# Graph network on one core: a landing wait, the place of a store, and the form of the one-hots

## What is computed

```python
# layer 0: Gaussian mixture convolution
gauss  = exp(sum(-0.5 * (attr - mu)**2 / (eps + sigma**2)))      # 3 weights per edge
msg    = einsum('eko,ek->eo', (x[src] @ g).reshape(E, 3, 64), gauss)
summed = segment_sum(msg, dst);  cnt = segment_sum(1, dst)
h      = summed / max(cnt, 1) + x @ root_w + bias
x      = layernorm(x + silu(h + x))
# layer 1: two SAGE convolutions over the same edges
h      = relu(x @ W_self1 + mean_of_neighbours(x) @ W_neigh1 + b1)
h      = h @ W_self2 + mean_of_neighbours(h) @ W_neigh2 + b2
out    = layernorm(x + h)
```

## The kernel before

| stretch | us | tiles q | counts are made by |
|---|---|---|---|
| first | 370 to 2099 | 0 to 29 | alternately two pairs a window (L1266, L1268), and merged (L1395, L1396) |
| second | 2099 to 2899 | 30 to 45 | one pair a window; many windows listed |
| third | 2899 to 3701 | 46 to 61 | one pair a window |
| fourth | 3701 to 5434 | 62 to 97 | merged; DVE also merges for the next tile (L1359 to L1376, with copies by ACT, L563) |

## Time and profile before

### The profile page before, as it was taken

How to read it: one execution, slowest core, us unless ns; L and a number is a source line. 1 busy time by engine, 2 the same in 40 slices (tenths; PEclk the granted TensorE clock), 3 DMA queues, 4 the chain that set the end, 5 groups by cost and what they waited for, 6 DMA issues and landing times.

```text
span 7415.5 us, 142564 instructions
## 1 busy us (share of the span) xinstructions
PE 4994.0 (67%) x35195; PEld 3986.1 (54%) x35196; DVE 4364.1 (59%) x15089; ACT 2698.4 (36%) x8317; POOL 3383.0 (46%) x3146
## 2 busy tenths in 40 slices
PE   1566666666655666666655555555645999999999
PEld 1223334443433444444444444444434999999999
DVE  5667888788877777676666665666634222222222
ACT  3113455454443455444455555555522000000000
POOL 5023666666665667677666666666610000000000
PEclk5557898888877888787777777788865999999999
DMA  2001222222222222222222222222220999999998
GB/s 74 28 25 48 92 75 91 86 79 75 91 73 89 82 101 92 74 92 92 79 89 93 93 93 93 93 75 93 93 67 35 368 381 381 382 369 386 384 385 342
DMA packets 258225, 1081.29 MB, mean 146 GB/s; under 512 B 140103, under 2 KB 144231, under 8 KB 194407
## 3 DMA queue, kind: packets, MB, share of 16 engines
q1 hardware_dynamic: 142806, 968.66, 33.9%
q0 software_dynamic: 100352, 102.96, 6.1%
q10 hardware_dynamic: 14902, 8.11, 0.5%
HBM read 751.67 MB, written 327.81 MB: 146 GB/s over the span
## 4 chain that ended last, share of the span: by engine, by line
PE 34%; POOL 20%; issue 16%; DVE 15%; DVEq 8%; DMA 4%; ACT 2%; SPq 0%; POOLq 0%; ACTq 0%
PE pw L968 21%; POOL rE L500 20%; PE pw L795 5%; DVE rE L1268 4%; DMA rE<-in_x,idx 3%; PE pw L820 2%; DVEq L1477 2%; DVEq L1301 2%; PE pw L767 2%; DVE rE L1266 2%; DVE rE L1328 1%; PE pw L935 1%; ACT rE L547 1%; DVEq L1253 1%; DVE rE L1396 1%
## 5 line engine op out<-in xcount | busy, mean ns | idle before, releaser
L500 POOL DMA_INDIRECT rE<-in_x,idx x3136 | 3380.8, 1078 | 2028.8 <-issue 1885.9
L795 PE MATMUL pw<-rE 128*128 128x193 f32 x7824 | 1708.9, 380 | 842.6 <-DVE rE L1328 805.7
L586 ACT CAST rB<-pw 128x792 bf16<-128x792 f32 x1568 | 1262.2, 813 | 2689.1 <-PE pw L820 1039.0
L795 PEld LDWEIGHTS pw<-rE 128*128 128x128 f32 x7824 | 1561.0, 225 | 1050.9 <-DVE rE L1328 986.3
L547 ACT ACTIVATE rE<-rE,cols 128x64 f32<-128x64 f32 x4704 | 1254.8, 344 | 8.0 <-DMA tab<-tab_d 8.0
L820 PE MATMUL pw<-rE 128*128 128x396 f16 x3840 | 813.1, 359 | 532.8 <-DVE rE L1268 389.7
L1268 DVE TENSOR_SCALAR rE<-iperm,gr 128x392 f16<-128x392 f16 x3840 | 1049.0, 313 | 0.0
L820 PEld LDWEIGHTS pw<-rE 128*128 128x128 f16 x3840 | 368.5, 103 | 915.8 <-DVE rE L1268 501.7
L968 PE MATMUL pw<-rE,rA 128*128 128x192 bf16 x9604 | 809.5, 246 | 0.1
L968 PE MATMUL pw<-rB,rA 128*128 128x192 bf16 x9604 | 809.2, 246 | 0.1
L968 PEld LDWEIGHTS pw<-rE,rA 128*128 128x128 bf16 x9604 | 789.7, 98 | 1.4
(11 more groups left out here) (257 smaller groups left out, 2615.7 us busy)
## 6 DMA issues: line engine op xcount, KB each, us to landing
rA<-count SPq DMA_DIRECT2D x392, 1568.0 KB, 8.4
count<-rB SPq DMA_DIRECT2D x98, 3136.0 KB
rE<-in_x,idx POOLq DMA_INDIRECT x3136
cols<-cols_d SPq DMA_DIRECT2D x98, 64.0 KB
cols_d<-rA SPq DMA_DIRECT2D x3, 1568.0 KB, 5.1
rA<-in_edge_attr ACTq DMA_DIRECT2D x1, 4608.0 KB
out<-gcol ACTq DMA_DIRECT2D x97, 32.0 KB, 6.1
count<-rB SPq DMA_DIRECT2D x8, 224.0 KB, 2.0
```

The costliest lines, as they stand in the source:

```text
L500: pool.indirect_dma_start(out=gath[:, s, u * CB + b, :], out_offset=None, in_=x, in_offset=bass.IndirectOffsetOnAxis(ap=idx[:, s, u * CB + ...
L586: act.copy(stage[:, s, :, j * 2 * W:(j + 1) * 2 * W].rearrange("p h (w n) -> p w h n", w=2), pu[j % 3][:, :, 0:CW].rearrange("p w (h n) -> ...
L795: ins = pe.matmul(sums[side][:, 0:AW], onehot[:, side, bb, :], wgath[:, side, bb, :], start=(bb == 0), stop=(bb == CB - 1))
```

## The change

Three edits.

1. POOL waits for landed rows once per tile, after chunk 3, and no more after chunk 1.
2. SP stores the counts of tile q last in its step: after weights, table and indices, and thus also after all gathers of tile q+1 have landed.
3. In the 68 tiles from q = 30 (`pairs_w == 1`, and `behind < 2` in the merged ones from q = 62) each one-hot set is made by eight `tensor_scalar`, each comparing `iota` with one value per partition. Tiles 0 to 29 keep the single instruction.

```diff
@@ sync @@
             for q in range(NT):
...
-                sp.wait_ge(a_evac, q * NU + (NU + 2))
                 sp.wait_ge(a_bnd, q + 1)
-                sp.dma_start(tile_of(count[part][0], ORDER[q] - PARTS[part][0]), stage[:, q % 2, None, 0:NT, :]).then_inc(a_st[q % 2], 16)
                 if q + 2 < NT:
                     sp.wait_ge(a_list, q + 1)
                     load_cols(q + 2)
-                if q + 3 < NT:
+                if q + 1 < NT:
                     for u in range(U):
                         sp.wait_ge(a_g[1 - q % 2][u], 16 * CB * ((q + 1) // 2 + 1))
+                if q + 3 < NT:
                     load_idx(q + 3)
+                sp.wait_ge(a_evac, q * NU + (NU + 2))
+                sp.dma_start(tile_of(count[part][0], ORDER[q] - PARTS[part][0]), stage[:, q % 2, None, 0:NT, :]).then_inc(a_st[q % 2], 16)
@@ gpsimd @@
-                        if u % 2:
+                        if u == U - 1:
                             pool.wait_ge(a_g[s][u], 16 * CB * (i + 1))
@@ vector @@
-            def prepare(t, s, u):
+            def prepare(t, s, u, apart=False):
...
-                    V.tensor_tensor(onehot[:, side], iota[:, None, :].broadcast_to([P, CB, P]),
-                                    local[:, :, None].broadcast_to([P, CB, P]),
-                                    ALU.is_equal).then_inc(a_oh[side], 1)
+                    if apart:
+                        for bb in range(CB):
+                            ins = V.tensor_scalar(onehot[:, side, bb, :], iota[:], local[:, bb:bb + 1], None, ALU.is_equal)
+                    else:
+                        ins = V.tensor_tensor(onehot[:, side], iota[:, None, :].broadcast_to([P, CB, P]),
+                                              local[:, :, None].broadcast_to([P, CB, P]), ALU.is_equal)
+                    ins.then_inc(a_oh[side], 1)
@@ merged_counts @@
-                            prepare(q, s, u)
+                            prepare(q, s, u, behind < 2)
@@ tile_counts @@
-                            prepare(q, s, u)
+                            prepare(q, s, u, pairs_w == 1)
```

## The result

The changed kernel takes 7461.66 us (median of 6 runs, 7455.13 to 7465.4) against 7431.97 before: ratio 1.004, 95% interval 1.003 to 1.0051. It is 30 us slower, where 33 us less was forecast; the change is 0.4%, small but clear of the interval. A second set of runs on another chip gave 1.0048 (1.0031 to 1.0065).

The account below looks back on a forecast made before the run. POOL's gathers were taken to bound the third and fourth stretches, DVE and PE the second, with DVE the bound after the change. Terms +41 - 17 - 57 = -33 us took the median from 7427.8 to 7395 us, range 7310 to 7480.

Parts of the forecast that it names:

- Now the sets: Step adding 0.57 us for each of 72, 77 and 202 one-hot sets to DVE's chain: +41, +44, +115 us.
- Edit 1 on POOL: Pause after chunk 1 falls from 2.77 to 0.30: 2.5 us per tile off POOL, 40 and 90 us in stretches three, four.
- Edit 3 on POOL: Gathers held less by one-hot sets: 1.1 us a tile gained on POOL, 18 and 40 us in stretches three and four.
- Edit 3 on DVE: Eight comparisons cost DVE +0.57 us a set: +0.44 for the instructions, +0.13 for gathers hitting them; bounds +0.3 to +1.4.
- DVE's chain without POOL's stalls: DVE's waits replaced by their unstalled values: 741 us in the third stretch, 1561 in the fourth, L1248 doubtful by 40 us.
- Fourth stretch: From tile 62, 36 tiles: DVE's 1676 us against POOL's 1603, so 1733 becomes 1676, -57 us.
- Second and third: Stretches from tiles 30 and 46: second +41 us to about 841, third -17 us, from 802 to 785.
- Edit 2: The store moved last in SP's step, costed at nothing; 14 us of gathers cover it before `stage` is needed.
- rival 3: Store comes too late and `stage` isn't free; with 3 us in each of 52 tiles 7551 us; chance 0.03.
- Rival 1: POOL stays the bound, DVE's chain ending before POOL's: -147 us, 7281; chance 0.13.
- Rival 2: Comparisons and gathers hold each other up; change turns slower at 0.66 us a set, 7511 at 0.9; chance 0.20.
- Which is late next: Step comparing DVE's and POOL's chains: DVE last in both, 785 against 744 (third stretch), 1676 against 1603 (fourth).

Follow-up runs that it names:

- single form: The changed kernel with edits 1 and 2 only, every one-hot set made by one instruction as before: 7286.89 us, ratio 0.9815 to before on an undisturbed chip.
- the lagged one: Kernel with edits 1 and 2 and old one-hots, but POOL's wait at a tile's end is for chunk 2's rows: 7211.27 us, ratio 0.9709.

## Why the prediction was wrong

**The missing term.** The step "Now the sets" counts on DVE's chain only the sets, and the sum +41 - 17 - 57 has no term for what seven instructions more in four calls do to the loop they stand in. It was put at nothing without a reason. The runs show in its place 3.2 us more at the loop's head in each pass, 101 us in all, and 117 us by the difference between 341 and 348 instructions. Without it the measured kernel would be near 7462 - 117 = 7345 (an estimate), some 87 us under before and 50 below the forecast; with it, it is 30 over before. It could have been found: the queue's row stands in the profile of before (139), the single-pair loop already waited 1.9 and 5.0 us at its head, and the order of instructions shows the length of the body.

Its other steps, one by one:

- *Edit 1 on POOL*, -2.5 us a tile. Right, -2.2: in the single form the tiles q = 66 to 95 start 45.9 us apart on POOL against 48.15 before, and the pause before chunk 2 is 0.30 or 0.31 in the tiles from q = 60 on.
- *Edit 3 on POOL*, -1.1 a tile. Right in kind: -0.8.
- *Edit 3 on DVE*, +0.57 a set. Direction right, size too large: the set's distance is 1.56 against 1.13, +0.43, and in time (1677 - 1595) / 202 = 0.41, (760 - 736) / 58 = 0.41 and 20 / 55 = 0.36. The 0.13 for gathers that hit comparisons isn't there in these differences.
- *DVE's chain without POOL's stalls*: 741 for the third stretch, measured 736; 1561 for the fourth, measured 1597 and 1595. L1248 was the doubtful term there, and it was the one: taken at 3.85 us each, it is 249.5 / 58 = 4.30 in the kernel whose POOL is far ahead (the lagged one), 26 of the 36 us.

```profile
DVE rA L1249 <- PE pw L796: 249.5, 58, 8.1
```

- *Fourth stretch*: 1676 forecast, 1675 and 1677 measured. It is right by luck, by two errors: 36 us too little for the chain and some 33 too much for the sets (202 x 0.16).
- *Second and third*: 841 and 785 forecast, 884 to 885 and 823 to 825 measured. Without the loads they would be near 824 and 768, so better than forecast.
- *Edit 2* at nothing: with the single form it gave some 25 us, between two chips. In the profile after no copy waits for a store, and rival 3 is out.
- *Rival 1*: out; POOL isn't the bound after the change. *Rival 2* (comparisons and gathers hold each other): its side of the result came true, its mechanism didn't; a set costs 0.4 us more, not 0.66. *Which is late next*: right, DVE and, with it, PE.

The sign was lost by a mechanism that stood in neither the sum nor the rivals. That 7462 lies inside the range of 7310 to 7480 is luck: the range ended at 7480 for another reason than the one that brought the time there.

## What to carry to other kernels

Before more instructions go into a hardware loop, count its body on that engine and look at the wait at its head and at the instruction queue's row: here seven instructions too many, 341 to 348, cost 3.2 us a pass at the loop's head, more than the new form of a tile's four or five sets (0.4 each). A change with several edits should be priced edit by edit: here the landing wait and the store together were worth -140 us, and the third edit took 175 back. When an engine loses the bound, its lead is worth something later: 29 us more in two stretches bought 60 in the next.

## What the hardware showed

- This loop of DVE stays loaded with 341 instructions, not with 348; beyond, 155 loads more (292 - 137) of 8.2 KB come in its 32 passes, about 5 a pass, and the head's wait rises from 1.9 / 5.0 to 5.1 / 8.2 us. Why it alternates, in the short loop too, was not looked into.
- Eight float32 comparisons of 128 columns with a value per partition take 1.56 us from start to start, one of 1024 columns with two inputs 1.13. Gathers are held less beside the former: their mean is 1.016 us in the fourth stretch, and 1.041 beside the latter.
- PE's granted clock in the second stretch is 0.76 with the loads (885 us) and 0.80 without (798 us), with the same matmuls (x2300 in both). That the longer gaps between them are the cause wasn't tested.
